# Gather stage of a graph layer: PE's three signals of a chunk on matmuls in place of a drain

## The reference, cut to what matters

```
# first layer
agg = segment_sum(x[src] * norm, etype * N + dst)
h   = relu(einsum(agg, W_rel) + bias + x @ loop_weight);  h = layernorm(x + h)
# second layer
e = (h[dst] - h[src]) @ theta.T + h[src] @ phi.T
e = relu(bn0(e));  e = e @ fc1.T;  e = relu(bn1(e))
x = segment_sum(e, dst) / maximum(cnt, 1)
out = layernorm(h + relu(x + h))
```

## Time and profile before

| | us |
|---|---|
| median of 3 runs | 3377.92 |
| lowest, highest | 3369.27, 3393.46 |
| the profiled execution | 3398.88 |
| its span, first to last instruction | 3397.0 |
| first gather stage, from about | 100 to 1331 |
| second gather stage, from about | 1455 to 2825 |

### The profile page before, as it was taken

One profiled execution on the slowest core, in us unless ns is written; L12 is line 12 of the kernel. 1 busy time (PEld: TensorE's weight loads), 2 busy tenths in 40 slices (PEclk: granted clock), 3 DMA queues, 4 the chain that ended last, 5 costly groups with the idle time before them and its releaser, 6 DMA issues. The chain is left out here.

```text
span 3397.0 us, 42692 instructions
## 1 busy us (share of the span) xinstructions
PE 1913.4 (56%) x10210; PEld 1481.2 (44%) x10211; DVE 1369.8 (40%) x3584; ACT 616.0 (18%) x1004; POOL 1602.3 (47%) x1759
## 2 busy tenths in 40 slices
PE   3455555555555555544443434444444448999997
PEld 3445455554545545422222222222222223479997
DVE  4233333333333333443332333333333336877776
ACT  2111111111111111310000000000000005744444
POOL 5655555555555553335555554555555550056001
PEclk7777777777777777755555555555555558999999
DMA  3111121212112111322222222222222226924443
GB/s 81 52 53 47 51 55 48 56 46 55 46 52 53 49 52 28 97 86 84 83 83 82 82 84 80 83 84 82 81 83 82 85 84 251 306 80 147 148 148 100
DMA packets 124078, 291.18 MB, mean 86 GB/s; under 512 B 34957, under 2 KB 77506, under 8 KB 106224
## 3 DMA queue, kind: packets, MB, share of 16 engines
q1 hardware_dynamic: 65856, 136.12, 12.5%
q0 software_dynamic: 50048, 102.50, 11.6%
q10 hardware_dynamic: 8112, 51.91, 4.0%
HBM read 227.22 MB, written 63.18 MB: 85 GB/s over the span
## 5 line engine op out<-in xcount | busy, mean ns | idle before, releaser
L697 POOL DMA_INDIRECT G<-btab,srcT x782 | 737.6, 943 | 735.3 <-POOLq L56 497.8
L682 POOL DMA_INDIRECT G<-in_x,srcT x782 | 742.7, 950 | 585.9 <-POOLq L56 356.7
L906 PE MATMUL PS<-ident,G 128*128 128x128 f32 x784 | 213.0, 427 | 770.7 <-issue 426.6
L906 PEld LDWEIGHTS PS<-ident,G 128*128 128x128 f32 x784 | 140.2, 217 | 864.3 <-issue 864.3
L1477 DVE TENSOR_SCALAR ohT<-PS,node_col 80x512 bf16<-80x512 f32 x196 | 146.2, 746 | 805.8 <-issue 448.2
L780 PE MATMUL PS<-BIG,G 128*128 128x192 f32 x1564 | 362.6, 397 | 68.4 <-PEq L56 53.3
L780 PEld LDWEIGHTS PS<-BIG,G 128*128 128x128 f32 x1564 | 331.6, 239 | 83.0 <-issue 82.8
L1046 ACT ACTIVATE BIG<-PS 128x768 f32<-128x768 f32 x196 | 158.3, 809 | 1143.4 <-ACTq L56 955.0
L1313 DVE SCALAR_TENSOR_TENSOR BIG<-PS,dst0T,BIG 128x192 f32<-128x192 f32 x784 | 324.1, 416 | 77.8 <-issue 67.9
L1101 ACT ACTIVATE BIG<-PS 128x512 f32<-128x512 f32 x196 | 117.0, 597 | 1258.7 <-ACTq L56 1206.8
L1322 DVE TENSOR_TENSOR ACC<-ACC,PS 128x24 f32 x782 | 135.2, 173 | 496.0 <-DVEq L56 352.2
(11 more groups left out here) (182 smaller groups left out, 1995.2 us busy)
## 6 DMA issues: line engine op xcount, KB each, us to landing
BIG<-spill SPq DMA_DIRECT2D x90, 1024.0 KB, 4.9
spill<-BIG ACTq DMA_DIRECT2D x49, 1024.0 KB
G<-in_x,srcT POOLq DMA_INDIRECT x782
G<-btab,srcT POOLq DMA_INDIRECT x782
typ_i<-in_edge_type SPq DMA_DIRECT2D x97, 128.0 KB
BIG<-atab SPq DMA_DIRECT2D x196, 60.0 KB
atab<-BIG SPq DMA_DIRECT2D x12, 384.0 KB
xn<-in_x SPq DMA_DIRECT2D x48, 64.0 KB
```

The costliest lines, as they stand in the source:

```text
L682: nc.gpsimd.indirect_dma_start(out=G[0:n, g % 2, t, :], out_offset=None, in_=x, in_offset=bass.IndirectOffsetOnAxis(ap=srcT[0:n, TPG * g + ...
L697: nc.gpsimd.indirect_dma_start(out=G[0:n, g % 2, t, :], out_offset=None, in_=btab[:, :], in_offset=bass.IndirectOffsetOnAxis(ap=srcT[0:n, ...
L906: pe.matmul(PS[:, 2 + k, q * TILE:(q + 1) * TILE], G[:, h, TPC * k + q, :], ident[:, :], start=(q == 0), stop=False, is_transpose=True, sk ...
```

## The change

PE no longer drains in this stage. `look_done` (or `look_first` in the wide version) is given by the chunk's last lookup matmul, `cnt_done` by its last count matmul, `d_ready` by the matmul that spreads the digits. The two increments that PE's sequencer made after the drain go. The order of the matmuls on PE, and all instructions of the other engines, stay as they were.

```diff
@@ spread_dst @@
                 pe.matmul(PS[:, k % 2, :], onesb[0:2, :], digits[:, h, k * CHUNK:(k + 1) * CHUNK],
-                          start=True, stop=True)
+                          start=True, stop=True).then_inc(d_ready, 1)
@@ edge_features @@
                         for a in range(3):
                             mm = pe.matmul(PS[:, 2 + k, :], aw[0:WIN, k, a, :], ohT[0:WIN, k % 2, :],
                                            start=False, stop=(a == 2), skip_group_check=True)
-                        if wide_chunks:
-                            mm.then_inc(look_first, 1)
+                        mm.then_inc(look_first if wide_chunks else look_done, 1)
 
                         take(pe, cnt_oh)
                         for q in range(TPC):
                             mm = pe.matmul(PS[:, 7, 0:NW], oh_lo[:, k % 2, q, :], oh_hi[:, k % 2, q, :], ...)
+                        mm.then_inc(cnt_done, 1)
...
                         if nxt:
                             spread_dst(*nxt)
-                        if wide_chunks:
-                            pe.drain().then_inc(cnt_done, 1)
-                        else:
-                            pe.drain().then_inc(look_done, 1)
-                            pe.sem_inc(cnt_done, 1)
-                        if nxt:
-                            pe.sem_inc(d_ready, 1)
...
             for k in range(2):
                 spread_dst(0, 0, 0, k)
-            pe.drain().then_inc(d_ready, 2)
```

## The result

The changed kernel took **3213.5 us** (median of four runs, 3210.24 to 3218.38) against 3375.7 for the kernel before (3369.27 to 3393.46): a ratio of **0.951**, 95% interval 0.947 to 0.955. A second measurement (experiment 2) gave 3214.1 against 3391.0, 0.948 (0.946 to 0.950). This is not the change's worth everywhere: where the kernel before takes 2602 to 2606 us, the changed kernel with one drain of each four put back, or with all four, stays within 0.1% of it (experiments 1, 2 and 6). The changed kernel itself has not run on such a chip.

What follows compares the result with a forecast made beforehand. Bound: POOL's 19.7 us of gather issue plus an 8.8 us gap from PE's held signals, 46 periods. Shorter gaps save 161 us and drains outside the bursts 7: 3377.9 - 168 = 3210 us, range 3150 to 3275 (8 in 10: 3095 to 3365).

Steps and rivals of the forecast that it cites:

- The main term: Second gather stage: PE no longer stops at a held signal, so the gap shrinks from 8.8 to 5.3 us, saving 161 us.
- The bound: Second gather stage: no engine's work binds; a period is 19.7 us of POOL's gather issue plus an 8.8 us gap.
- POOL-bound: Rival: the new signals escape the hold, the gap falls to 0.3 us, 398 us less, 2980 us; chance 0.10.
- Is it the drain that is slow?: Claimed no: in the first gather stage, without drains, increments on matmuls are held to the same two moments.
- the 6.7 us gap for the fourth: Second gather stage: one group in four has chunk 3's spread held to the burst's end, giving a 6.7 us gap.
- Drains outside the cover: Some ten chunks at the second gather stage's start and end, outside POOL's bursts, save 0.7 us each, 7 us.
- Sequencer increments at nothing: 390 PE sequencer increments move onto matmuls; costed at nothing, bounds 0 and the 0.7 us a chunk already counted.
- SP's windows at nothing: SP's window loads, 20.76 us for four issues in a burst, costed at nothing because issued some chunks ahead.
- the period of 27.7: Second gather stage: the period SP's window loads would set without their cover, 4 x 6.9 us; a sign of being wrong.
- The increments' tail: About 26 ns for each further matmul increment; 10 us later if all 392 lay on the path.
- Serial: Rival: PE issues too slowly behind held matmuls, gap 7.1 to 7.9 us, 3293 to 3330 us; chance 0.16.
- Slower: Rival: the pile behind the hold grows, every group gets the 11.55 us gap, +120 us, 3498 us; chance 0.10.

Runs made afterwards that it cites:

- experiment 2: Changed kernel again, against the kernel before: 3214.1 us against 3391.0, ratio 0.948; on a 2602 us chip, drains without signal after every chunk 0.9993, POOL taking by chunk 0.9971.
- experiments 1, 2 and 6: Changed kernel with drains without signal put back, against the kernel before: every chunk 0.9996 and 0.9993, chunk 1 alone 0.9998, chunk 3 alone 0.9994, chunk 2 alone 0.9992.
- experiment 3: Changed kernel with several ways by stretch in one run: as changed 24.16 us a period, as before 27.33, drains without signal 26.80, short pause 23.75, long pause 23.95.
- e1: Changed kernel with a drain without signal put back after every chunk, signals kept on matmuls: 0.9996 of the kernel before on a 2605.8 us chip.
- experiment 5: Changed kernel with POOL taking one buffer return before each chunk's gathers in both gather stages: 3051.6 us against 3315.7 for the kernel before, ratio 0.920.
- experiment 4: Ways by stretch, us a period: changed 24.38; with silent drain after chunk 0 24.14, chunk 2 26.13, chunks 1 and 3 24.27; 32-row gathers 24.56; before, POOL by chunk 24.0.

## Why the prediction was right

Forecast 3210, measured 3213.5; the period 25.0 forecast, 24.67 measured. The mechanism is the forecast one: PE issues on behind a held signal, and the held copies come as a pair. That the time is hit within 4 us is partly luck. The savings were taken from a profiled execution 21 us above the median and subtracted from the median; the same comparison with the profile after gives 188.6 us where 168 were forecast, and the medians give 162.2. The main term, too small by 16, and that excess offset each other. Point by point:

- **The bound.** Right for this chip: POOL's issue plus a gap that PE's held signals set. The gap was 8.8 and is 24.67 - 19.66 = 5.0. What I did not see is that the hold is not there on every chip. Without it the kernel before takes 2606 us, and the rival "POOL-bound" is what every kernel does there.
- **"Is it the drain that is slow?"** No, as argued from the first stage: a silent drain after each chunk costs nearly as much as one that signals (26.80 and 27.33 us a group), and drains put into the first stage cost it 2.6 a group.
- **The main term**, 161 us: 177.5 in the profile. PE's issue of chunk 3 ahead of the burst's end, which I gave three groups in four, came in all but one of the 46; the 6.7 us gap for the fourth does not occur there, and in experiment 2 it occurs twice (gaps of 6.54 and 6.46). The usual gap is 5.0 and not 4.8, since the copies are 1.06 us apart and not 0.8, and about ten gaps are 3.7 to 4.4, where chunk 2 was out earlier. One group came late (a gap of 9.9, behind one of 2.3).
- **Which chunk the stop is worth.** The prediction argued from chunk 1's drain, because in the kernel before it is chunk 1 that is caught. With the other drains gone chunk 1 is over 4.3 us into the burst and its drain ends within it, at a cost of at most 0.5 us; chunk 2 is the one that is caught. The catch moves with the pace, and a price read from one chunk before does not hold after.
- **Drains outside the cover**, 7 us: the stage's end gave 6.8 (38.1 against 31.3 from the last burst's start to the last copy), its start, from POOL's first gather to its first restart, 2.0. A drain and its signals cost 0.57 us where nothing is held, against 0.7 taken from the earlier trace rows.
- **Sequencer increments at nothing**: 0.53 us a period between silent drains and drains with the signals (experiment 3), which would be 24 us over the stage. Six periods a side don't prove it, and it is not told apart from `look_done` being given 0.6 us earlier. Whether this step was too low stays open.
- **SP's windows at nothing**: right. PE waited for a window 13 times in the stage, 10.6 us in all, 1.5 at most, and the period of 27.7 did not come.
- **The increments' tail**, 10 us by "TensorE: Matmul & The Clock Gate" (The cost: per-tile semaphore tail) of the Trainium skill: no row shows it. PE is busy 3.16 us a chunk after (581.82 / 184) and 3.07 before (564.64 / 184), and hardly a record is missing (2215 and 2209 for 2208 matmuls). But the matmuls that now give a signal are no longer by their records: 602 ns for the spread against 603, 226 for the count in both, 618 for the lookup against 634. With all three signals on the matmuls and the drains kept (e1) it is 3.07 (573.42 / 187). The ends are modelled, so this does not rule a tail out.
- **The rule of the Trainium skill** ("PSUM — Partial Sum Buffer", Engine vs sequencer instructions: an increment on a matmul fires when it completes) agrees with the 2606 us chips, where a copy starts 0.25 us after the end of the lookup's record (1505.54 + 1.49, then 1507.28, in e1). On holding chips the increment of a lookup that the record has over at 2017.93 came at 2033.26. Whether the completion or its signal is late no row shows.
- **Rivals.** Serial: copies 1.06 us apart and not 3, out. Slower: the release does not get later with what is issued behind, about 23.0 us from a burst's start before and after.

## What to carry to other kernels

While one engine runs a long burst of indirect transfers, let the others keep issuing: a drain is cheap where nothing holds its signal (0.6 us), and it stops the engine until the release where it waits behind the burst (14 us of standstill, 1.75 us more a group). Which one that is has to be tried, one drain at a time. Let a gathering engine take back its buffer in small pieces, not a whole group at once; in the second stage that alone brought a period to 24.0 us, against 24.4 for the change alone and 23.5 for both, and it was the only edit that helped on the 2606 us chips too, by 0.3%. Before a gain is credited, run the kernel before on more than one chip: here it takes 2606 us on one and 3391 on another, and on the first kind putting the drains back costs nothing that can be measured.

## What the runs showed of the hardware

- **Chips, or the states they are in, differ.** The kernel before took 2602 to 2606 us on three chips and 3313 to 3391 on three, at the same 943 to 946 ns a gather, with the same clock of 0.50 in the second gather stage and with the same bytes. What makes a chip hold was not found.
- **The records differ with it.** The six traces with the hold carry 6637 to 7708 records of semaphore updates by landed transfers, the eight without it 33297 to 33622, though the whole kernels move the same 124078 to 124080 packets. Nor has e1 any stop of 1.7 us within its gathers: the longest gap between two is 0.32 us. Every time in this document is of an execution whose span and clock were recorded, so a rival stands untested: that the hold comes from the recording, and would not be there without it.
- **The release counts gathers.** On holding chips signals that come after some 5 us of a burst are let out at 11.45 us after its start for 8 gathers (experiment 3's long pause, start 2363.11), 17.3 for 12 (experiment 5, start 1513.85) and 22.8 to 23.0 for 16: 1.43 us a gather, while POOL issues one each 1.25. With 32 rows, issued each 1.17 us, it is 22.7 for 16 all the same. The one burst of 24 (experiment 4, start 2087.30) gives 33.3, which is 1.39 each.

```profile
2374.56 0.75 DVE L1514 TENSOR_SCALAR ohT<-PS,node_col 80x512 bf16<-80x512 f32 x1 [5.53 <-DVEq L68]
```
```profile
1531.12 0.75 DVE L1469 TENSOR_SCALAR ohT<-PS,node_col 80x512 bf16<-80x512 f32 x1 [7.07 <-DVEq L56]
```

- It looks as if something works off each gather in about 1.4 us and PE's signals wait for it, most of them until it has caught up. It is not the moving of the rows: in the kernel after, the packets of the last gather end 20.8 to 21.1 us after the start of every burst of 16, two us ahead of the release, and with 32 rows 19.3 to 19.6, over three us ahead. The reading fits the numbers and was not tested; some signals do come out within a burst, such as the one at 2023.23 in the kernel after, 13 us into it.
- A pause of POOL in the burst, 4 us after 8 gathers, does away with the gap at the end (23.95 us a period, 4 of them the pause). The short pause, 1.24 us, does nearly as well (23.75), with 3.1 us left at the end. So the wait can be moved, but little of it is saved.
